# Moving GpSimd's row transfers behind the context of the next batch, in a gated cross-attention and linear kernel on one core

## Chip, cores and metric

One core of one Trainium2 chip runs the whole kernel. The metric is the device time of an execution in microseconds. TensorE is PE in the profile, VectorE is DVE, ScalarE is ACT, GpSimd is POOL and SyncE is SP.

## What is computed

All arrays are float32 but the packed weight. x has 8 batches of 100 rows of 2048, the context 8 batches of 722 rows of 2048. The weight has 2048 rows of 1536 int32 words, three words for four 6-bit values.

```
a = einsum(layernorm(x), ctx)            # per batch: 100 x 722 scores
c = einsum(softmax(a), ctx)              # 100 x 2048
x = x + tanh(g_xattn) * c
w = (unpack6(qweight) - zero_point) * scale
y = einsum(layernorm(x), w) + bias       # 800 rows x 2048 x 2048
out = x + tanh(g_ffn) * y
```

## The kernel before

The first part runs over the 8 batches, the second over 4 column blocks of the weight with 7 row tiles each. Every engine has its instruction order written out by hand, with semaphores between them.

**The batches.** The context of a batch is six tiles of up to 128 rows in `raw[:, b % 2]`, 5.9 MB together, so the context of batch b goes where that of batch b-2 was. `scores(b)` on TensorE has 32 steps f = 0 to 31: it transposes a 128-column piece of three context tiles (fill f of kind "S"; steps 0 to 15 use tiles 0 to 2, steps 16 to 31 tiles 3 to 5), and three steps later multiplies the piece, split by ScalarE (L421) and VectorE (L666) into two parts, with the queries. `attend(i)` multiplies the probabilities with the context, tile by tile (t = 0 to 5, eight matmuls each), and counts `s_pvt` after each of the first five. SyncE waits for that count and then loads the same tile of batch i+2 (L233), the last one after `s_pv`. Between the tiles t = 4 and t = 5 of `attend(i)` stand the transposes of the queries of batch i+2 (`queries`, halves (0, 1) before t = 4 and (2, 3) before t = 5). For one i the order on TensorE is `scores(i+1)`, `probs(i)`, `attend(i)`.

**The rows of x.** One buffer `xa` holds the rows of x to be normalized as queries, one buffer `xres` the rows of x to which the attention is added, one buffer `rows` the centred and scaled result for the second part. GpSimd moves them all on its own queue (q0), 800 KB a time: `next_x(b)` fetches x[b] to `xa` once the queries of batch b-1 are transposed; `x1_out(i)` sends `xres` once `residual(i)` is done; `next_xres(i)` fetches x[i] to `xres` once `x1_out(i-1)` has landed and `ln2_center(i-1)` has read it; `rows_out(i)` sends `rows`, `rs_out(i)` a column of 100 single floats. Between them it computes the reciprocal square roots (`rstd`, six small instructions).

**VectorE** in round i: `residual(i-1)`, `context_lo(i+1)` (the splits of the scores), `row_max(i+1)`, `ln2_stats(i-1)` (waits for nothing new), `ln2_center(i-1)` (L569; it writes `rows`, and so waits until `rows_out` of all batches up to i-2 has landed: `dve.wait_ge(s_rowsout, 16 * i)` within `ln2_center(i)`), `ln1_stats(i+2)` (waits for x[i+2]), `coef`, `ln2_scale(i-1)` (L575), `ln1_norm(i+2)` (L537, waits for the reciprocal square root from GpSimd), `queries_lo(i+2)`.

**The passage to the second part.** In round 6 (LAST - 1) there is no batch i+2. In its place `attend(6)` has the transposes of row tiles 0 and 1 (`normed`, "x" fills) before t = 1 to 4 and of weight tile 0 (`weights(0)`, L836) before t = 5. They share two PSUM banks; a bank is free again when VectorE has done `rows_lo` for it (L588). `unpack(n)` (L607 to L612) turns the packed words of weight tile n, loaded by SyncE (L257), into values.

Of the kernel before, what the change touches and what calls it, by code (L numbers as in the profile page):

```python
# [19 lines left out]
def flamingo_block(nc, x, ctx_in, g_xattn, g_ffn, qweight, wscale, wzero, wbias, out):  # L20
# [8 lines left out]
    CH = D // P  # L29
# [7 lines left out]
    LAST = B - 1  # L37
# [17 lines left out]
    with ExitStack() as stack:  # L55
# [3 lines left out]
        def psum(name, shape):  # L59
            return stack.enter_context(nc.psum_tensor(name, shape, F32))  # L60

        def sem(name):
            return stack.enter_context(nc.semaphore(name))
# [49 lines left out]
        S = psum("S", [P, 2, 512])  # L113
# [24 lines left out]
        s_turned = [sem(f"s_turned{k}") for k in range(4)]  # L138
# [77 lines left out]
        def bank(kind, i, f):  # L216

            return FILL[kind, i, f]
# [102 lines left out]
        @block.gpsimd  # L321
        def _(pool):
            pool.memset(ident[:, :], 0.0).then_inc(s_id0, 1)
            pool.memset(ident16[:, :], 0.0).then_inc(s_id0, 1)
            pool.memset(half[:, :], -0.5).then_inc(s_half, 1)
            pool.wait_ge(s_id0, 2)
            for m in (ident, ident16):
                pool.affine_select(out=m[:, :], in_=m[:, :], compare_op=ALU.not_equal, fill=1.0,
                                   base=0, pattern=[[-1, P]], channel_multiplier=1).then_inc(s_id, 1)
            pool.memset(fold[:, :], 0.0).then_inc(s_fold, 1)  # L330
            for k in range(STRIPS):
                pool.wait_ge(s_fold, k + 1)
                pool.affine_select(out=fold[:, :], in_=fold[:, :], compare_op=ALU.not_equal, fill=1.0,
                                   base=-32 * k, pattern=[[-1, 32]], channel_multiplier=1).then_inc(s_fold, 1)
            pool.wait_ge(s_half, 1)
            done = [0]

            def rstd(k, b):

                q = done[0]  # L340
                done[0] += 1
                vt, y0, a, c = (ln[0:R, k, i:i + 1] for i in range(4))
                to = X_SCALE if k else 1.0
                pool.wait_ge(s_aggr[k], b + 1)
                pool.tensor_scalar(vt, mr[0:R, k, 1:2], EPS, None, ALU.add).then_inc(s_var, 1)
                pool.wait_ge(s_var, q + 1)
                pool.tensor_tensor(y0, vt, half[0:R, :], ALU.pow).then_inc(s_pow, 1)
                pool.wait_ge(s_pow, q + 1)
                pool.tensor_tensor(a, y0, y0, ALU.mult).then_inc(s_nt, 1)
                pool.wait_ge(s_nt, q * 3 + 1)  # L350
                pool.tensor_tensor(a, a, vt, ALU.mult).then_inc(s_nt, 1)
                pool.wait_ge(s_nt, q * 3 + 2)
                pool.tensor_scalar(c, a, -0.5 * to, 1.5 * to, ALU.mult, ALU.add).then_inc(s_nt, 1)
                pool.wait_ge(s_nt, q * 3 + 3)
                pool.tensor_tensor(mr[0:R, k, 1:2], y0, c, ALU.mult).then_inc(s_rstd[k], 1)

            def next_x(b):
                f = bank("q", b - 1, 3)
                pool.wait_ge(s_turned[f[0]], f[1] + 1)
                pool.dma_start(xa[0:R, :], x[b]).then_inc(s_xa, 16)  # L360

            def x1_out(i):
                pool.wait_ge(s_x1, i * NCH + NCH)
                pool.dma_start(x1_dram[i], xres[0:R, :]).then_inc(s_x1out, 16)

            def rs_out(i):
                pool.wait_ge(s_rs, i + 1)
                if i == LAST:
                    pool.wait_ge(s_rsout, 16 * LAST)
                pool.dma_start(rs_dram[i * R:(i + 1) * R, :], rsum[0:R, i % 2:i % 2 + 1]).then_inc(s_rsout, 16)  # L370

            def rows_out(i):
                pool.wait_ge(s_rows, i + 1)
                pool.dma_start(rows_dram[i * R:(i + 1) * R, :], rows[0:R, :]).then_inc(s_rowsout, 16)

            def next_xres(i):
                pool.wait_ge(s_x1out, 16 * i)
                pool.wait_ge(s_mid, i)
                pool.dma_start(xres[0:R, :], x[i]).then_inc(s_xres, 16)

            rstd(0, 0)
            pool.dma_start(xres[0:R, :], x[0]).then_inc(s_xres, 16)
            next_x(1)
            rstd(0, 1)
            for i in range(B):
                if i + 2 < B:
                    next_x(i + 2)
                if i >= 1:
                    x1_out(i - 1)
                    rstd(1, i - 1)  # L390
                if i + 2 < B:
                    rstd(0, i + 2)
                if i >= 1:
                    next_xres(i)
                    rows_out(i - 1)
                    rs_out(i - 1)
            x1_out(LAST)
            rstd(1, LAST)
            rows_out(LAST)
            rs_out(LAST)  # L400
# [120 lines left out]
        def _(dve):  # L521
# [18 lines left out]
            def row_max(b):  # L540
                dve.wait_ge(s_scores, b + 1)
                dve.tensor_reduce(soft[0:R, b % 2, 0:1], S[0:R, :, 0:GW], AX.XY, ALU.max, negate=True).then_inc(s_nmax, 1)
# [9 lines left out]
            def residual(i):  # L552
                dve.wait_ge(s_xres, 16 * i + 16)
                dve.wait_ge(s_coef, i + 1)
                for n in range(NCH):
                    dve.wait_ge(s_pv, i * NCH + n + 1)
                    piece = xres[0:R, n * 512:(n + 1) * 512]
                    dve.scalar_tensor_tensor(out=piece, in0=pv[n][0:R, :], scalar=soft[0:R, i % 2, 3:4], in1=piece,
                                             op0=ALU.mult, op1=ALU.add).then_inc(s_x1, 1)
# [21 lines left out]
            def rows_lo(m, half):  # L581

                r = MROWS[m]
                for f in (2 * half, 2 * half + 1):
                    k, u = bank("x", m, f)
                    dve.wait_ge(s_hi, 4 * m + f + 1)
                    hi, lo = (xT[m][:, h, 4 * f:4 * f + 4, :] for h in range(2))
                    dve.tensor_tensor(lo, T[k][:, :].rearrange("p (c r) -> p c r", r=r), hi, ALU.subtract).then_inc(s_free[k], 1)  # L588
# [7 lines left out]
            def unpack(n):  # L596

                dve.wait_ge(s_w[n % 2], 16 * (n // 2) + 16)
                if n == 0:
                    dve.wait_ge(s_pvt, (LAST - 1) * (NT - 1) + 3)  # L600
                if 2 <= n < 2 * RT + 2:
                    k, u = bank("W", n - 2, 1)
                    dve.wait_ge(s_turned[k], u + 1)
                elif n >= 2 * RT + 2:
                    dve.wait_ge(s_wn, n - 2 - 2 * RT + 1)
                p = wraw[n % 2].bitcast(U16).rearrange("p (g w h) -> p g w h", w=3, h=2)
                dve.tensor_scalar(unp[n % 2][:, 1, :], p[:, :, 0, 0], 6, 63, ALU.logical_shift_right,  # L607
                                  ALU.bitwise_and).then_inc(s_u1, 1)
                for j, w in ((0, 0), (2, 1), (3, 2)):
                    dve.tensor_scalar(unp[n % 2][:, j, :], p[:, :, w, 0], 63, 0x6400, ALU.bitwise_and, ALU.bitwise_or)  # L610
                dve.wait_ge(s_u1, n + 1)
                dve.tensor_scalar(unp[n % 2][:, 1, :], unp[n % 2][:, 1, :], 0x6400, None, ALU.bitwise_or).then_inc(s_u, 1)  # L612
# [67 lines left out]
            for i in range(B):  # L680
                if i >= 1:
                    residual(i - 1)
                if i < LAST:
                    context_lo(i + 1, {})
                    row_max(i + 1)
                if i >= 1:
                    ln2_stats(i - 1)
                    ln2_center(i - 1)
                if i + 2 < B:
                    ln1_stats(i + 2)  # L690
                if i < LAST:
                    coef(i + 1)
                    if i >= 1:
                        ln2_scale(i - 1)
                if i + 2 < B:
                    ln1_norm(i + 2)
                    queries_lo(i + 2)
                elif i < LAST:
                    rows_lo(0, 0)
                    rows_lo(0, 1)  # L700
                    scale_and_bias()
                    unpack(0)
                    rows_lo(1, 0)
                    unpack(1)
                    rows_lo(1, 1)
            unpack(2)
            rows_lo(2, 0)
            ln2_scale(LAST - 1)
# [232 lines left out]
```

## Time and profile before

| what | value |
|---|---|
| time before, median of 3 runs | 670.11 us (667.25 to 682.67) |
| the profiled execution's own time | 668.26 us |
| its span | 666.5 us |
| PE busy | 607.7 us, 91% of the span |
| DVE, ACT, POOL busy | 392.8, 195.7, 58.2 us |
| granted TensorE clock, mean | 0.972 |
| DMA | 113.64 MB, mean 171 GB/s |

The span begins with the first instruction of the program and ends with the last, so 1.8 us of the profiled execution lie outside of it. Busy time of an engine is what its instructions took; PEld is TensorE's weight load, which overlaps its matmuls. The granted clock is the share of TensorE's full 2.4 GHz that it was given.

### The profile page before, as it was taken

The numbers are of one execution on the slowest core, as the hardware profiler recorded it, in microseconds if no ns is written. First come the engines' busy times: TensorE is split into PE (matmuls) and PEld (weight loads), VectorE is DVE, ScalarE is ACT, GpSimd is POOL, SyncE is SP. The second block draws the span as 40 slices with busy tenths as digits, with TensorE's granted clock in tenths as the row PEclk, the third lists the DMA queues.
The fourth block names the chain that finished last, engine by engine and source line by source line (L and its number), as shares of the span: only waits on it lengthen the run. The fifth ranks groups of instructions, "written<-read, shape, count | busy, mean of one in ns | idle before, by whom it ended". The sixth has DMA issues, their size and how long they took to land.

```text
span 666.5 us, 8134 instructions
## 1 busy us (share of the span) xinstructions
PE 607.7 (91%) x3240; PEld 392.1 (59%) x3240; DVE 392.8 (59%) x687; ACT 195.7 (29%) x391; POOL 58.2 (9%) x149
## 2 busy tenths in 40 slices
PE   0978999999699699969959998989999999999997
PEld 0877947947665694756559478445466444444443
DVE  2575636666375456728536675957676776563543
ACT  1544514514332350422235044223232131121000
POOL 3000000030013003001200300201200000000000
PEclk9997999999799899979989999989999999999999
DMA  8993058059829607912950692676843499394220
GB/s 250 273 285 101 1 162 282 12 180 255 308 68 305 181 0 217 266 71 87 302 165 1 226 299 106 210 220 185 285 157 83 143 252 253 90 247 106 83 68 35
DMA packets 39618, 113.64 MB, mean 171 GB/s; under 512 B 20974, under 2 KB 20974, under 8 KB 29422
## 3 DMA queue, kind: packets, MB, share of 16 engines
q1 hardware_dynamic: 18718, 83.54, 40.6%
q0 software_dynamic: 4224, 25.40, 12.7%
q10 hardware_dynamic: 16640, 4.20, 3.8%
q8 instruction: 25, 0.41, 0.3%
q14 instruction: 11, 0.09, 0.0%
HBM read 89.26 MB, written 19.66 MB: 163 GB/s over the span
## 4 chain that ended last, share of the span: by engine, by line
PE 77%; DMA 19%; DVE 2%; ACT 1%; SPq 1%; issue 1%; DVEq 0%
PE pv L812 24%; DMA raw<-in_ctx 17%; PE pv L863 17%; PE S L793 9%; PE S L863 8%; PE T L754 8%; PE S L795 5%; PE pv L754 4%; DMA raw<-in_L_ffn_qweight 2%; PE T L836 1%; PE S L876 1%; PE pv L876 1%; SPq L233 0%; ACT pT L435 0%; DVE stats L524 0%
## 5 line engine op out<-in xcount | busy, mean ns | idle before, releaser
L812 PE MATMUL pv<-raw,pT 128*100 128x512 f32 (+1 forms) x384 | 171.6, 597 | 2.5 <-ACT pT L436 2.5
L793 PE MATMUL S<-khi,qT 128*100 128x362 f32 x512 | 146.3, 368 | 0.0
L812 PEld LDWEIGHTS pv<-raw,pT 128*100 128x100 f32 (+1 forms) x384 | 62.3, 168 | 89.6 <-issue 85.8
L666 DVE TENSOR_TENSOR klo<-T,khi 128x361 fp32r<-128x361 f32 x128 | 67.7, 533 | 68.5 <-ACT khi L421 67.9
L754 PE MATMUL T<-ident,raw 128*128 128x128 f32 (+1 forms) x384 | 64.6, 284 | 31.7 <-DMA raw<-in_ctx 30.6
L421 ACT ACTIVATE khi<-T 128x361 fp32r<-128x361 f32 x128 | 60.0, 473 | 98.0 <-PE T L754 97.8
L795 PE MATMUL S<-klo,qT 128*100 128x362 f32 x256 | 87.3, 341 | 0.6 <-DVE klo L666 0.6
L666 DVE TENSOR_TENSOR klo<-pv,khi 128x361 fp32r<-128x361 f32 x128 | 67.6, 533 | 33.6 <-ACT khi L421 33.4
L754 PEld LDWEIGHTS T<-ident,raw 128*128 128x128 f32 (+1 forms) x384 | 52.3, 150 | 40.9 <-issue 37.3
L421 ACT ACTIVATE khi<-pv 128x361 fp32r<-128x361 f32 x128 | 60.0, 475 | 41.8 <-PE pv L754 41.3
L793 PEld LDWEIGHTS S<-khi,qT 128*100 128x100 f32 x512 | 71.6, 175 | 0.1
L863 PE MATMUL pv<-raw 128*128 128x512 f16 x288 | 64.0, 379 | 0.0
L754 PE MATMUL pv<-ident,raw 128*128 128x128 f32 (+1 forms) x384 | 61.7, 274 | 0.0
L754 PEld LDWEIGHTS pv<-ident,raw 128*128 128x128 f32 (+1 forms) x384 | 51.3, 146 | 3.4
L414 ACT ACTIVATE qT<-T 128x400 fp32r<-128x400 f32 x32 | 14.7, 501 | 114.9 <-PE T L754 114.9
L863 PEld LDWEIGHTS pv<-raw 128*128 128x128 f16 x288 | 28.1, 98 | 32.4
L795 PEld LDWEIGHTS S<-klo,qT 128*100 128x100 f32 x256 | 44.0, 172 | 2.5 <-DVE klo L666 2.1
L656 DVE TENSOR_TENSOR qT<-T,qT 128x400 fp32r<-128x400 f32 x32 | 17.2, 571 | 43.7 <-ACT qT L414 43.5
L754 PE MATMUL T<-ident,xa 100*128 100x100 f32 (+2 forms) x192 | 24.5, 274 | 17.8 <-DVE xa L537 14.8
L754 PEld LDWEIGHTS T<-ident,xa 100*128 100x128 f32 (+2 forms) x192 | 22.6, 172 | 27.7 <-issue 23.4
L863 PE MATMUL pv<-raw,extra 128*128 128x512 f16 x160 | 35.0, 379 | 0.0
L647 DVE TENSOR_TENSOR raw<-pv,extra 128x512 f32<-128x512 f32 (+1 forms) x18 | 12.4, 688 | 31.0 <-PE pv L863 31.0
(88 smaller groups left out, 539.7 us busy)
## 6 DMA issues: line engine op xcount, KB each, us to landing
raw<-in_ctx SPq DMA_DIRECT2D x32, 1024.0 KB, 13.4
raw<-in_ctx SPq DMA_DIRECT2D x16, 840.0 KB, 14.9
raw<-in_L_ffn_qweight SPq DMA_DIRECT2D x16, 768.0 KB, 6.5
xres<-in_x POOLq DMA_DIRECT2D x8, 800.0 KB, 8.8
x_scratch<-xres POOLq DMA_DIRECT2D x8, 800.0 KB, 14.8
rows_scratch<-rows POOLq DMA_DIRECT2D x8, 800.0 KB, 12.6
raw<-x_scratch SPq DMA_DIRECT2D x24, 256.0 KB, 4.1
out_y<-raw SPq DMA_DIRECT2D x24, 256.0 KB, 2.5
```

Source lines behind the costliest of these rows:

```text
L414: act.activation(qT[:, 0, 4 * f:4 * f + 4, :], T[k][:, 0:4 * R].rearrange("p (c r) -> p c r", r=R), ACT.Copy).then_inc(s_qhi, 1)
L421: act.activation(khi[:, (b * 2 * CH + f) % RING, 0:GW], T[k][:, 0:GW], ACT.Copy).then_inc(s_khi, 1)
L647: dve.tensor_tensor(o[0:r, :], ACC[j % NA][0:r, :], scB[0:r, cols], ALU.mult).then_inc(s_mul, 1)
L656: dve.tensor_tensor(qT[:, 1, 4 * f:4 * f + 4, :], T[k][:, 0:4 * R].rearrange("p (c r) -> p c r", r=R), qT[:, 0, 4 * f:4 * f + 4, :].bitcas ...
L666: dve.tensor_tensor(klo[:, slot, 0:GW], T[k][:, 0:GW], khi[:, slot, 0:GW].bitcast(F32), ALU.subtract).then_inc(s_free[k], 1)
L754: last = pe.transpose(dst(T[k]), src, ident[0:n, 0:n])
L793: pe.matmul(S[0:R, g, 0:MW], qT[:, h, c, :], khi[:, slot, :], start=(c == 0 and h == 0), stop=False)
L795: last = pe.matmul(S[0:R, g, 0:MW], qT[:, 0, c, :], klo[:, slot, :], start=False, stop=(c == CH - 1))
L812: last = pe.matmul(pv[n][0:R, :], pT[0:ROWS[t], t, :], raw[0:ROWS[t], b % 2, t, n * 512:(n + 1) * 512], start=(t == 0), stop=(t == NT - 1))
L836: last = pe.transpose(T[k][:, :].bitcast(F16)[:, (c % 8) * P:(c % 8 + 1) * P], unp[n % 2][:, q, gb * P:(gb + 1) * P].bitcast(F16), ident16 ...
L863: last = pe.matmul(ACC[j % NA][0:r, :], xT[m][:, h, c, :], WT[nb % 2][:, c, :], start=(c == 0 and h == 0), stop=(c == CH - 1 and h == 1))
L876: last = pe.matmul(ACC[j % NA][32 * k:32 * k + TAIL, :], xT[MT - 1][:, h, c + k, :], WT[nb % 2][:, c + k, :], start=(c == 0 and h == 0), s ...
```

## The change

GpSimd gets a wait, `context_there(b)`, until TensorE has made the transposes of fill 16 (CH is 16) of the context of batch b, the first that read the tiles 3 to 5. It stands at the head of every round i below 7, for batch i+1, ahead of `next_x(i + 2)`. `rows_out` moves from the end of its round to the next round, behind `x1_out`, for batches 0 to 4; those of 5, 6 and 7 stay in their rounds. `next_xres(i)` moves ahead of `rstd(0, i + 2)`. On VectorE the second half of `rows_lo` of row tile 1 moves ahead of `unpack(1)`.

```diff
+            def context_there(b):
+                k, u = bank("S", b, CH)
+                pool.wait_ge(s_turned[k], u + 1)
...
             for i in range(B):
+                if i < LAST:
+                    context_there(i + 1)
                 if i + 2 < B:
                     next_x(i + 2)
                 if i >= 1:
                     x1_out(i - 1)
+                if 2 <= i < LAST:
+                    rows_out(i - 2)
+                if i >= 1:
                     rstd(1, i - 1)
+                    next_xres(i)
                 if i + 2 < B:
                     rstd(0, i + 2)
+                if i >= LAST - 1:
+                    rows_out(i - 1)
                 if i >= 1:
-                    next_xres(i)
-                    rows_out(i - 1)
                     rs_out(i - 1)
...
                     unpack(0)
                     rows_lo(1, 0)
+                    rows_lo(1, 1)
                     unpack(1)
-                    rows_lo(1, 1)
```

## Rows read from the trace of the kernel before

**Rows 1.** The page's chain that ended last, by engine.

```profile
PE 77%; DMA 19%; DVE 2%; ACT 1%; SPq 1%; issue 1%; DVEq 0%
```

**Rows 2.** Waits of PE: engine, line, waited for, us in total, times, longest.

```profile
PE T L754 <- DMA raw<-in_ctx: 30.6, 6, 7.0
```

**Rows 3.** Windows between `attend` starts: us, busy by engine, granted clock, DMA share, GB/s.

```profile
85.61:134.69 49.08, 48.77 (x265) 34.95 (x263) 26.89 (x50) 18.32 (x43) 2.78 (x8) 1.00 0.47 155
...
306.55:364.77 58.22, 50.89 (x265) 36.62 (x263) 33.21 (x59) 18.32 (x42) 7.42 (x17) 0.94 0.52 158
364.77:416.60 51.83, 48.95 (x265) 34.86 (x263) 33.13 (x59) 18.32 (x42) 6.89 (x16) 1.00 0.63 203
sum 330.99, PE 301.37 PEld 216.22 DVE 192.66 ACT 109.94 POOL 39.34; mean PE 50.23 PEld 36.04 DVE 32.11 ACT 18.32 POOL 6.56
```

**Rows 4.** Timeline of PE in `scores`: start, us; idle before and releaser in brackets.

```profile
224.60 0.47 PE L754 MATMUL pv<-ident,raw 128*128 128x128 f32 x3
231.19 0.84 PE L754 MATMUL T<-ident,raw 128*128 128x128 f32 x3 [5.62 <-DMA raw<-in_ctx]
...
401.66 0.50 PE L754 MATMUL T<-ident,raw 128*128 128x128 f32 x3 [2.57 <-DMA raw<-in_ctx]
```

**Rows 5.** DMA issues by windows (56, 108, 204 and 213.5 us): KB, us to landing.

```profile
xa<-in_x POOLq DMA_DIRECT2D x1, 800.0 KB, 5.2
...
raw<-in_ctx SPq DMA_DIRECT2D x1, 840.0 KB, 8.3
...
rows_scratch<-rows POOLq DMA_DIRECT2D x1, 800.0 KB, 15.3
rs_scratch<-rsum POOLq DMA_DIRECT2D x1, 0.4 KB, 16.5
...
raw<-in_ctx SPq DMA_DIRECT2D x1, 840.0 KB, 16.9
```

**Rows 6.** Windows chosen for the DMA rate, columns as in rows 3.

```profile
111.00:114.00 3.00, 3.00 (x25) 2.92 (x24) 2.18 (x5) 1.67 (x5) 0.00 (x0) 1.00 0.93 257
210.00:215.00 5.00, 5.00 (x28) 2.87 (x25) 3.85 (x7) 1.58 (x4) 0.54 (x1) 1.00 0.99 401
215.50:222.50 7.00, 7.00 (x54) 6.77 (x54) 5.07 (x11) 4.17 (x10) 0.26 (x1) 1.00 0.91 151
229.20:236.00 6.80, 4.81 (x20) 4.51 (x21) 1.49 (x3) 1.42 (x3) 0.00 (x0) 0.50 0.03 10
...
424.50:431.00 6.50, 6.50 (x28) 3.79 (x27) 5.40 (x9) 1.99 (x4) 0.79 (x2) 1.00 0.92 289
432.50:439.00 6.50, 5.86 (x20) 2.65 (x18) 1.66 (x5) 1.08 (x2) 0.00 (x0) 1.00 1.09 150
```

**Rows 7.** Timeline of one round (i = 2), PE, DVE and POOL.

```profile
188.45 0.47 PE L754 MATMUL pv<-ident,raw 128*128 128x128 f32 x3
...
194.64 2.35 DVE L569 TENSOR_SCALAR_CACHE_REDUCE rows<-xres,mr 100x2048 f32<-100x2048 f32 x1
...
199.42 0.26 DVE L526 BATCH_NORM_AGGREGATE mr<-stats 100x2 f32<-100x24 f32 x1
...
204.71 0.54 POOL L370 DMA_DIRECT2D rs_scratch<-rsum  x1
...
210.82 0.54 POOL L360 DMA_DIRECT2D xa<-in_x  x1 [5.58 <-PE T L754]
...
215.22 0.54 POOL L364 DMA_DIRECT2D x_scratch<-xres  x1 [3.86 <-DVE xres L558]
```

**Rows 8.** Timeline of round 6, around the first weight tile.

```profile
434.76 3.60 PE L812 MATMUL pv<-raw,pT 128*100 128x512 f32 x8
437.96 0.50 DVE L607 TENSOR_SCALAR raw<-raw 128x512 uint16<-128x512 uint16 x1 [4.84 <-DMA raw<-in_L_ffn_qweight]
...
440.63 1.69 PE L836 MATMUL T<-ident,raw 128*128 128x128 f16 x16 [2.27 <-DVE extra L588]
...
442.11 4.70 PE L812 MATMUL pv<-raw,pT 105*100 105x512 f32 x8
```

## The prediction, made before the changed kernel was run

> **What bounds the kernel now.** I read the chain of waits first: TensorE holds 77% of it and DMA 19%, nobody else more than 2% [rows 1]. The list of PE's waits then names the DMA: 30.6 us in six waits for the context, the longest 7.0 us [rows 2]. To see where they lie I cut the batch part into windows from the start of one `attend` to the start of the next [rows 3]. The reader is to compare them: every window has the same 265 matmuls, the first takes 49.08 us, the fifth 58.22, the sixth 51.83. The timeline shows what the long ones hold [rows 4]: TensorE does 16 steps of `scores`, finds tiles 3 to 5 not there at step 16, and stands still for 5.62 us (7.0 in the worst window, 2.57 in the sixth). After the longer stops the granted clock is 0.50 for 6.8 us, 1.2 GHz instead of 2.4 [rows 6]; after the 2.57 us stop it stays 1.00 through its window [rows 3, 4].
>
> What an undisturbed round costs follows from the sixth window: 51.83 - 2.57 = 49.26 us, with the row work of VectorE in it. The sum of all six is 330.99 [rows 3]; less the first (49.08) this is 281.91, and five undisturbed rounds are 246.3. So **35.6 us** hang on late tiles, clock included: for the fifth, 58.22 - 49.26 = 9.0, of which 7.0 standing and 2.0 slow clock.
>
> Why are the tiles late? The last tile of the context comes 16.9 us after its issue in a late round and 8.3 us in the round with no wait, and 5.2 is what 800 KB need alone [rows 5]. TensorE reaches step 16 some 12.2 us after the start of `scores` (213.4 to 225.6, [rows 4]). Two things lie in the way. GpSimd's queue has xres, rows, xa and x_scratch in flight exactly then (issued up to 215.2, the last two at 210.8 and 215.2, [rows 7]), 3.3 MB beside the context's 5.9 MB. And for 7 us the DMA engines are as busy as before (0.91) but move 151 GB/s instead of 401 [rows 6]. That stretch comes when the 100 single floats of `rs_out` are under way, issued at 204.71 and landed 16.5 us later [rows 5, 7]. I put it on them and not on the `scores` phase, since it comes again at 432.5 to 439 within an `attend` (150 GB/s), and is missing in the `scores` of the first round, which has no `rs_out` (257 GB/s) [rows 6].
>
> **The change part by part.** The new wait ends at step 16 of `scores(i+1)`, by when all six tiles have landed. I count from there. Fifteen more steps of 0.81 us end at 12.2; `ln2_center`, the first to need anything, starts 194.64 - 188.92 = 5.7 us after the last transposes [rows 7], at 17.9.
>
> *The wait and what is queued behind it.* Behind it on GpSimd stand `next_x`, `x1_out`, `rows_out` and then the square roots, which need VectorE's statistics from after `scores` anyway. The three issues take 0.54 us each [rows 7], from 0.3 to 1.9. Lower bound for the third landing: 5.2 us for the first, and two more at 289 GB/s, the rate of two queued transfers [rows 5, 6], 2 x 2.8: 11.1. Upper bound: issued at 1.4 and as slow as the slowest shown, 15.3 [rows 5]: 16.7. I take 12, near the low end, since the context is all in and the queue is alone. Both ends are ahead of 17.9, so the new dependence of `ln2_center(i-1)` on `rows_out(i-2)` costs nothing; its cover is 1.2 to 6.8 us. If it were gone, each us would shift the query transposes, with little slack of their own. x[i+2] lands first and is needed later still. In round 0 x[2] is fetched later than before too, and needed as late as in the others. In round 2 the three broadcast loads of 1 MB go out behind context 3 on SyncE's queue; they are through within some 8 us (3.1 MB at 401 GB/s), about when the three transfers start.
>
> *What leaves the context's way.* x, x1 and rows, 2.5 of the 3.3 MB, go into a stretch of idle DMA. What remains is `next_xres(i)`. It now goes right after `ln2_center` has read xres (194.64 + 2.35 = 197.0 in the round of rows 7; before, some 1.7 us ahead of the issue at 204.71), and `rs_out` right behind the square root of x[i+2], at some 203.0. The single floats then follow 0.8 MB instead of 1.6 MB and no x1 or x. So the slow stretch moves from 215.5 to 222.5 to about 205 to 212, into `attend`. Tiles 0 to 2 (3.0 MB) must land by 213.4, the end of `attend`. By 205 the context has 1.8 to 2.4 MB in (8 us at 289 to 401 GB/s, less 0.8 for xres), in the slow stretch 1.06 MB more (7 us at 151): 2.9 to 3.4. So tile 2 lands between in time and, if it needs what follows the stretch, 1 us late. I take 0.5 us in five rounds: **+2.5** (0 to 5). Tiles 3 to 5: at 212 at most 3.1 MB are missing, 7.7 us at 401; with the usual 1 us for landing, 221, against a need at 225.6. So no wait at step 16, and no fall of the clock. The whole **35.6 us** go.
>
> The Trainium skill (DMA: Bandwidth & Descriptors, Specifications) says that transfers under 512 bytes are read-modify-write; it does not say that they slow others. If the slow stretch were not theirs but that of `scores`, it would stay at 215.5, with 1.3 MB left then: 8 us at 151 GB/s, in time too; the sum would lose its +2.5.
>
> *`next_xres` ahead of `rstd(0)`.* Its issue takes up to 1.2 us, and ends before VectorE has the statistics of x[i+2], 199.42 against 197.0 + 1.2 [rows 7]. Nothing on the path; xres lands long before `residual`.
>
> *Rounds 6 and 7.* The sends of round 5 keep their place, and `rows_out(4)` lands before `ln2_center(5)` as above. Nothing.
>
> *VectorE's exchange.* Before, TensorE ended tile t = 4 at 438.36 and stood 2.27 us until `rows_lo(1, 1)`, which stood behind `unpack(1)`, which waited 4.84 us for the weight [rows 8]. Now `rows_lo` goes 4 us earlier, and `unpack(1)` waits as before, 0.65 us later if at all, with weight tile 1 needed only in the next `attend`. After its stop TensorE had the half clock: 4.70 us instead of 3.60 for eight matmuls and some 0.6 more on the transposes [rows 8]. Together **3.9 us** (2.3 to 3.9, if the clock falls anyway).
>
> **Sum.** 668.26 - 35.6 - 3.9 + 2.5 = 631.3 us against the profiled execution; its own 668.26 is 1.9 below the median of the three runs, so I say **632 us**, 5.7% faster.
>
> **The rivals.**
> (1) *The wait moves to the start of `scores`.* The single floats now slow the first tiles. If xres and the floats take all of the DMA from 198 to 212, tile 2 comes 3 us late in five rounds, and the clock falls in each (2 us): 631.3 - 2.5 + 25 = 654. For it: 1.8 MB at the low end is only just enough. Against: 300 GB/s and more in `attend` otherwise.
> (2) *The x traffic was not the cause.* The sixth window has no fetch of x and no late rows, and still waits 2.57 us. If as much stays in five rounds: 644. Against: there the slow stretch still lay on tiles 3 to 5, and now moves away.
> (3) *Slower: GpSimd's burst ends after `ln2_center` wants it.* VectorE then holds back x[i+2] and the queries, and TensorE stands in `attend` with a fallen clock. It decides from a third landing at 17.9 plus 1.5 us of slack. To cost more than the 39.5 us gained, five rounds would have to lose 8 us each (6 standing and 2 clock), a third landing at 25: three transfers at about 105 GB/s. Only if the burst itself brings on the slow rate: some 680 us at 27. Against: 289 GB/s for two such transfers in a row.
> (4) *The change doesn't do what it says*, because the wait ends early: it can't, since step 16 reads the tiles that it stands for. Part of (2).
>
> **Chances.** Forecast (624 to 641) 0.72, (2) 0.10, (1) 0.14, (3) 0.02, and something better, a round below 49.26 us, 0.02. The range from 624 to 648 takes in the forecast's unknowns (+2.5 at 0 to 5, the exchange's 1.6, some 3 us from execution to execution) and (2); it leaves out (1) and (3). About 2% is what a measurement tells from no change, 13 us here, which all but (3) exceed: faster 0.95, same 0.03, slower 0.02.
>
> **What would show it.** The list of waits should have only the first load of PE's waits for the context; windows from `attend` to `attend` of 49 to 50 us with the clock at 1.00; issues of xa, x_scratch and rows_scratch one behind the other in the middle of `scores`; landing of the context's last tile 6 to 9 us after issue; the low-rate stretch in the middle of `attend`; no wait of L836 for L588. It would be wrong if a wait stands before the first transposes of `scores` (1), at step 16 (2), or before the query transposes (3).

## The result, and the profile after

The changed kernel took 636.8 us (median of 4, 631.6 to 648.2) against 669.7 us before: a ratio of 0.950, 95% interval 0.937 to 0.962. Run twice more on other occasions it gave 0.946 (0.941 to 0.951) and 0.944 (0.938 to 0.951), with medians of 638.7 and 639.7 us where the kernel before took 676.6 and 677.2 us. Medians are of all executions of a kernel, ratios leave out those that are over 1.5% above the fastest of it. The forecast was 632 us, range 624 to 648, a ratio of 0.943.

The execution that was profiled first (648.2 us) has two waits of 5.3 and 7.6 us in the second part for weight tiles transposed by DMA, which the two later profiles of the same kernel don't have; what lengthened them isn't shown. So I read the later one of 637.4 us span, and call it the second profile.

The page's chain that ended last, of the second profile:

```profile
PE 83%; DMA 13%; DVE 1%; ACT 1%; SPq 1%; issue 1%; DVEq 0%
```

The waits of PE, in the same profile (us in total, times, longest):

```profile
PE T L765 <- DVE xa L548: 15.6, 1, 15.6
PE T L765 <- DMA raw<-in_ctx: 10.8, 6, 5.8
```

30.6 us of waiting for context have become 10.8 [rows 2]. Of these, 2.8 before and 6.7 now are the first load, ahead of any round (the 5.8 is part of it): in the rounds 27.8 us have become 4.1. DMA's share of the chain goes from 19% to 13% [rows 1]. The wait of L836 for L588 is gone. Windows from the start of one `attend` to the next, as in rows 3, with the granted clock and the DMA rate last:

```profile
92.42:141.51 49.09, 48.78 (x263) 34.97 (x263) 26.88 (x50) 18.30 (x43) 2.77 (x8) 1.00 0.48 155
141.51:191.75 50.24, 48.96 (x262) 34.84 (x262) 33.18 (x59) 18.29 (x43) 7.77 (x17) 1.00 0.80 247
191.75:242.47 50.72, 48.97 (x263) 34.87 (x263) 33.19 (x59) 18.30 (x43) 7.77 (x17) 1.00 0.61 182
242.47:291.93 49.46, 48.98 (x263) 34.86 (x263) 33.18 (x59) 18.29 (x43) 7.79 (x17) 1.00 0.63 187
291.93:342.10 50.17, 48.96 (x262) 34.85 (x262) 33.19 (x59) 18.30 (x43) 7.79 (x17) 1.00 0.64 184
342.10:392.13 50.03, 48.96 (x262) 34.88 (x262) 33.18 (x59) 18.30 (x43) 7.25 (x16) 1.00 0.71 210
392.13:418.55 26.42, 26.11 (x102) 13.37 (x103) 20.95 (x37) 7.98 (x17) 3.70 (x9) 1.00 0.78 215
```

The first window is as before; the next five were 56.5, 57.2, 58.2, 58.2 and 51.8 us and are now 49.5 to 50.7, with the clock at 1.00 throughout. Their sum is 250.6 instead of 281.9. The last line is round 6 with the first weight tile: 26.42 us, where the kernel before has this, from its own `attend(6)` to its `attend(7)`:

```profile
417.13:447.65 30.52, 27.94 (x103) 14.30 (x103) 20.83 (x37) 7.98 (x17) 3.72 (x9) 0.94 0.77 226
```

So 31.3 + 4.1 us are gained, the second part takes the same 218.8 us in both, and 6.3 us are lost in the first 92 us (the first `attend` starts at 92.4 instead of 86.1), where both kernels do the same: TensorE waits 3.9 us longer for the first load, and the granted clock of the stretch is 0.93 instead of 0.96. In the third profile it starts at 85.8, so this changes from execution to execution.

**The three transfers.** The timeline of POOL from `attend(2)` into the next `scores` (start us, us), and under it the landings of the DMAs issued between 227.5 and 229 us (KB, us to landing):

```profile
202.71 1.47 POOL L375 DMA_DIRECT2D rs_scratch<-rsum  x1
227.81 0.55 POOL L365 DMA_DIRECT2D xa<-in_x  x1 [23.63 <-PE T L765]
228.35 0.53 POOL L369 DMA_DIRECT2D x_scratch<-xres  x1
228.87 0.53 POOL L379 DMA_DIRECT2D rows_scratch<-rows  x1
```

```profile
xa<-in_x POOLq DMA_DIRECT2D x1, 800.0 KB, 6.3
x_scratch<-xres POOLq DMA_DIRECT2D x1, 800.0 KB, 8.0
rows_scratch<-rows POOLq DMA_DIRECT2D x1, 800.0 KB, 9.6
```

They go out one behind the other in the middle of `scores`; the third lands at 228.87 + 9.6 = 238.5, 10.6 us after the first issue. The reader sees where it is needed in VectorE's timeline, which starts L580 (`ln2_center`, L569 before) 6.9 us later, with no wait in front:

```profile
244.99 0.27 DVE L537 BATCH_NORM_AGGREGATE mr<-stats 100x2 f32<-100x24 f32 x1
245.38 2.35 DVE L580 TENSOR_SCALAR_CACHE_REDUCE rows<-xres,mr 100x2048 f32<-100x2048 f32 x1
```

**What is left.** TensorE still waits, not at step 16 of `scores` but at its first transposes:

```profile
164.72 0.50 PE L765 MATMUL T<-ident,raw 128*128 128x128 f32 x3 [0.98 <-DMA raw<-in_ctx]
215.42 0.82 PE L765 MATMUL T<-ident,raw 128*128 128x128 f32 x6 [1.44 <-DMA raw<-in_ctx]
```

The low-rate stretch has moved with the single floats, as the windows of DMA rate show (GB/s last):

```profile
203.00:209.00 6.00, 6.00 (x22) 2.82 (x21) 2.13 (x3) 0.90 (x2) 1.19 (x1) 1.00 1.00 354
210.00:216.00 6.00, 4.56 (x21) 2.16 (x20) 3.87 (x6) 0.94 (x3) 0.00 (x0) 1.00 0.62 91
```

So 354 GB/s until 209, then 91 until 216. The floats were issued at 202.7. GpSimd's queue moves 24 packets under 512 bytes between 208 and 210 and none from 210 to 217: the low rate follows on the small packets and doesn't run beside them. The third context tile (index 2) was issued just before them, and these are its landing (window 202.2 to 202.6) and theirs:

```profile
raw<-in_ctx SPq DMA_DIRECT2D x1, 840.0 KB, 12.8
```

```profile
rs_scratch<-rsum POOLq DMA_DIRECT2D x1, 0.4 KB, 12.6
```

202.33 + 12.85 (the tile's time in the chain) = 215.2 and 202.71 + 12.6 = 215.3: tile and floats land together, and TensorE, ready for the tile, stood for 1.4 us. By 209 the context queue had moved some 3.3 MB, more than the 3.0 MB of tiles 0 to 2. So a count of bytes doesn't explain the late tile. Whether its last packets or only the word of their arrival came late isn't shown.

### The profile page after: what moved, and what is told of

It reads as the page before. It is cut to its first block, busy times and chain, and to the rows that moved or that the text cites. A ratio compares the mean times of both kernels' runs of the same rounds, so it can differ in the third digit from the quotient of the medians.

```text
span 646.4 us, 8141 instructions
## 1 busy us (share of the span) xinstructions
PE 601.2 (93%) x3240; PEld 385.5 (60%) x3240; DVE 392.9 (61%) x687; ACT 195.7 (30%) x391; POOL 60.1 (9%) x149
## 4 chain that ended last, share of the span: by engine, by line
PE 81%; DMA 16%; DVE 1%; ACT 1%; SPq 1%; issue 1%; DVEq 0%
PE pv L823 19%; PE pv L874 17%; PE S L804 12%; DMA raw<-in_ctx 12%; PE T L765 9%; PE S L874 8%; PE S L806 6%; PE pv L765 6%; DMA raw<-xa 3%; PE T L847 1%; PE S L887 1%; PE pv L887 1%; SPq L233 1%; ACT pT L446 0%; DVE stats L535 0%
## 5 line engine op out<-in xcount | busy, mean ns | idle before, releaser
L804 PE MATMUL S<-khi,qT 128*100 128x362 f32 x512 | 142.8, 360 | 0.0
L806 PE MATMUL S<-klo,qT 128*100 128x362 f32 x256 | 85.8, 335 | 0.6 <-DVE klo L677 0.6
L804 PEld LDWEIGHTS S<-khi,qT 128*100 128x100 f32 x512 | 69.6, 170 | 0.1
L765 PE MATMUL T<-ident,raw 128*128 128x128 f32 (+1 forms) x384 | 61.9, 275 | 7.3 <-DMA raw<-in_ctx 6.1
L765 PEld LDWEIGHTS T<-ident,raw 128*128 128x128 f32 (+1 forms) x384 | 50.6, 145 | 15.9 <-issue 12.5
L806 PEld LDWEIGHTS S<-klo,qT 128*100 128x100 f32 x256 | 42.7, 167 | 2.3 <-DVE klo L677 2.0
L874 PE MATMUL pv<-raw,extra 128*128 128x512 f16 x160 | 36.8, 392 | 7.6 <-DMA raw<-xa 7.6
L477 ACT ACTIVATE xa<-raw 128x2048 f16<-128x2048 f16 x8 | 15.3, 1910 | 63.0 <-DVE raw L623 63.0
```

The source lines that it names most:

```text
L477: act.activation(wn[n % 2], unp[n % 2].rearrange("p j g -> p (j g)").bitcast(F16), ACT.Copy, bias=-float(BIAS16)).then_inc(s_wn, 1)
L765: last = pe.transpose(dst(T[k]), src, ident[0:n, 0:n])
L804: pe.matmul(S[0:R, g, 0:MW], qT[:, h, c, :], khi[:, slot, :], start=(c == 0 and h == 0), stop=False)
L806: last = pe.matmul(S[0:R, g, 0:MW], qT[:, 0, c, :], klo[:, slot, :], start=False, stop=(c == CH - 1))
L874: last = pe.matmul(ACC[j % NA][0:r, :], xT[m][:, h, c, :], WT[nb % 2][:, c, :], start=(c == 0 and h == 0), stop=(c == CH - 1 and h == 1))
```

## The experiments

Ratios are against the kernel before, run on the same chip in the same job, with 95% intervals.

**after_again** and **after_third**: the changed kernel again.

> The changed kernel as it is, for a profile without the long transposes of the second part and for a closer ratio. My theory: 632 us, ratio 0.944 (0.935 to 0.955), windows from attend to attend of 49 to 50 us with the granted clock at 1.00; the waits at the start of the second weight block (5.3 and 7.6 us in the first profile) were an accident of that execution. Rival: these waits come with the change, because the second part now starts at another moment; then 645 us, and they stand in this profile too.

> The changed kernel again, beside the three others on this chip, for comparison: 632 us, ratio 0.944.

Measured 0.946 (0.941 to 0.951) and 0.944 (0.938 to 0.951). The waits in the second part are in neither profile. The third profile shows how much the waits at the start of `scores` vary, here in three of its rounds:

```profile
134.89:187.57 52.68, 50.41 (x262) 36.33 (x263) 33.30 (x59) 18.50 (x43) 7.77 (x17) 0.97 0.79 235
...
239.22:289.80 50.58, 48.98 (x262) 34.88 (x262) 33.20 (x59) 18.29 (x43) 7.79 (x17) 1.00 0.65 183
289.80:344.00 54.20, 50.44 (x262) 36.14 (x262) 33.21 (x59) 18.30 (x43) 7.78 (x17) 0.97 0.64 170
```

The waits in these rounds are 2.0, 1.3 and 3.5 us, and behind the first and the last the granted clock is 0.50 for three to four us. So the half clock has not gone for good with the change.

**swap_only**: VectorE's exchange alone.

```diff
                     rows_lo(1, 0)
+                    rows_lo(1, 1)
                     unpack(1)
-                    rows_lo(1, 1)
```

> The kernel before with only VectorE's exchange: rows_lo(1, 1) ahead of unpack(1). My theory: no wait of L836 for L588 in round 6, 2.3 to 3.9 us less, ratio 0.994 to 0.997. Rival: the wait moves to the next weight load and nothing is gained, ratio 1.000.

Measured 0.995 (0.991 to 0.998), 3.6 us less at 669, as expected and just clear of no change. Its round 6:

```profile
424.75:451.16 26.41, 26.11 (x102) 13.36 (x102) 20.76 (x37) 7.97 (x17) 3.71 (x9) 1.00 0.80 202
```

26.41 against 30.52: 4.1 us, with the clock at 1.00 instead of 0.94. The wait for L588 is gone and no other came. This profile also shows how much the kernel before varies: its five rounds with waits take 287.6 us together, where those of rows 3 take 281.9.

**wait_only**: the new wait alone, in the kernel before.

```diff
             for i in range(B):
+                if i < LAST:
+                    context_there(i + 1)
                 if i + 2 < B:
                     next_x(i + 2)
```

> The kernel before with only the new wait at the head of GpSimd's round: x and x1 move behind the context, rows_out, next_xres and rs_out stay where they were. My theory: 1.6 MB leave the context's way, the slow stretch of the single floats stays at the start of scores; the last tile lands 9 to 11 us after its issue, just about in time: 0 to 2 us of waiting per round, 632 + 4 to 646 us, ratio 0.950 to 0.965. Rival (the x traffic was not the cause, the single floats were): the wait at step 16 stays at some 5 us, 660 us, ratio 0.985.

Measured 0.961 (0.955 to 0.967), in my range but with less gained than its middle; the rival's 0.985 is excluded. Its waits of PE:

```profile
PE T L761 <- DMA raw<-in_ctx: 16.4, 6, 3.3
PE T L843 <- DVE extra L595: 3.3, 1, 3.3
```

Without the first load these are 13.4 us in five rounds, 2.7 each at step 16, more than the 0 to 2 expected; the second line is what the exchange takes away.

**late_wait**: the changed kernel with the wait at the last transposes of the context.

```diff
-                k, u = bank("S", b, CH)
+                k, u = bank("S", b, 2 * CH - 1)
```

> The changed kernel with the wait 15 steps later, at the last transposes of the context (fill 31 in place of 16), so that the cover of the three transfers is gone. My theory: the third transfer lands about 12 us later, 6 us after ln2_center could start; with 1.5 us of slack the query transposes come 5 us late and the clock falls (2 us) in four rounds, and 2 to 3 us in round 6: 660 us (650 to 672), all the gain but 10 us given back, ratio 0.985. Rival (the moment does not matter as long as the context is in): 632 us, ratio 0.945.

Measured 0.989 (0.983 to 0.996): most of the gain is given back. The profiled execution took 676.5 us, the three others 664.7 to 669.5. Its timelines of DVE and PE in round 3 show the mechanism; the second PE line is of round 4, the third of round 6:

```profile
262.49 2.35 DVE L580 TENSOR_SCALAR_CACHE_REDUCE rows<-xres,mr 100x2048 f32<-100x2048 f32 x1 [7.74 <-DMA rows_scratch<-rows]
```

```profile
271.96 1.26 PE L765 MATMUL T<-ident,xa 100*128 100x100 f32 x6 [6.01 <-DVE xa L548]
328.41 0.93 PE L765 MATMUL T<-ident,xa 100*128 100x100 f32 x4 [4.98 <-DVE xa L548]
...
435.19 0.98 PE L765 MATMUL T<-ident,xa 128*128 128x128 f32 x5 [2.07 <-DVE extra L599]
```

`ln2_center` waits 7.7 us for `rows_out`, and TensorE 5.3, 6.0, 5.0 and 6.5 us for the queries in the four rounds (2.1 in round 6). The four waits are 22.8 us together. So the dependence that the change creates is real, and hidden by the place of the wait.

**order_only**: the changed kernel without the new wait.

```diff
             for i in range(B):
-                if i < LAST:
-                    context_there(i + 1)
                 if i + 2 < B:
```

> The changed kernel without the new wait: rows_out a batch later, next_xres earlier, VectorE's exchange, but x and x1 fetched and sent as early as before. My theory: x, x1 and rows (2.5 MB) now all lie on tiles 4 and 5; they wait 2 to 5 us at step 16 in most rounds, with a fall of the clock: 645 to 662 us, ratio 0.965 to 0.99. Rival (the gain came from the slow stretch alone, which this kernel moves too): 632 to 636 us, ratio 0.95.

Measured 0.958 (0.949 to 0.966), a little better than expected. It waits both at the start of `scores` and at step 16, in some rounds at both:

```profile
PE T L763 <- DMA raw<-in_ctx: 16.7, 7, 3.4
```

Beside after_third (0.944, same job) the wait itself is worth 1.4%, some 9 us; the two intervals just overlap, and every execution of after_third is faster than every one of order_only, the closest by 1.3 us.

**before_singles** and **after_singles**: the kernel before, and the changed one, with the single floats of batches 0 to 6 in one transfer after batch 6.

```diff
-        rsum = sb("rsum", [P, 2])
+        rsum = sb("rsum", [P, B])
...
-                pool.dma_start(rs_dram[i * R:(i + 1) * R, :], rsum[0:R, i % 2:i % 2 + 1])
+                if i == LAST - 1:
+                    pool.dma_start(rs_dram[0:LAST * R, :].rearrange("(b r) o -> r (b o)", r=R), rsum[0:R, 0:LAST], ...)
```

> The kernel before, with the single floats of batches 0 to 6 sent in one transfer after batch 6 and no longer in each round (the sums are kept in eight columns; all is still computed). My theory: the stretch of 150 GB/s at the start of scores is gone, the last context tile lands 10 to 12 us after its issue, in time or nearly: 633 to 645 us, ratio 0.95 to 0.965. Rival (the slow stretch belongs to scores or to the x traffic, not to the single floats): it stays, 668 us, ratio 1.00.

> The changed kernel with the single floats of batches 0 to 6 in one transfer after batch 6. My theory: the low rate in the middle of attend goes, tile 2 is in time, the two waits of 0.7 and 1.0 us at the start of scores go: 630 us, ratio 0.942, within 2 us of the changed kernel. Rival (the single floats do nothing): the low-rate stretch stays and the time is the same as that of the changed kernel.

Measured 0.952 (0.945 to 0.960), as expected, and 0.924 (0.915 to 0.933), better than the 0.942 that I expected: I took the floats' cost in the changed kernel from the two short waits of the first profile. The 0.924 rests on two executions, 625.2 and 626.1 us; the two others took 640.5 and 644.4, for a reason that no profile shows. In before_singles `attend(2)` starts 4.3 us earlier than in the kernel before, so the stretch that had 151 GB/s [rows 6] corresponds to this one, with 256:

```profile
211.20:218.20 7.00, 7.00 (x54) 6.77 (x54) 5.07 (x11) 4.19 (x10) 0.26 (x1) 1.00 0.93 256
```

The waits for context are halved, from 30.6 to 14.3 us. In after_singles no round waits any more; all five are 49.05 to 49.09 us, and only the first load is left in the list:

```profile
230.97:280.06 49.09, 48.79 (x262) 34.94 (x262) 33.20 (x59) 18.29 (x43) 6.43 (x16) 1.00 0.57 188
280.06:329.14 49.08, 48.77 (x262) 34.93 (x262) 33.20 (x59) 18.30 (x43) 6.43 (x16) 1.00 0.57 188
...
PE T L766 <- DMA raw<-in_ctx: 1.7, 1, 1.7
```

The 700 floats, once sent together in the last round, make a low-rate stretch there, 46 GB/s for 7 us (8 in all by windows of 1 us, and 9 in before_singles) and 411 after it, under work that does not wait:

```profile
422.00:429.00 7.00, 7.00 (x36) 3.40 (x34) 4.68 (x8) 3.80 (x4) 0.00 (x0) 1.00 0.92 46
430.00:434.00 4.00, 4.00 (x27) 2.11 (x26) 3.70 (x8) 0.00 (x0) 0.71 (x2) 1.00 0.99 411
```

**after_double**: the floats sent twice.

```diff
                 pool.dma_start(rs_dram[i * R:(i + 1) * R, :], ...).then_inc(s_rsout, 16)
+                if i < LAST:
+                    pool.dma_start(rs_copy[i * R:(i + 1) * R, :], ...).then_inc(s_rscopy, 16)
```

> The changed kernel, with the single floats of batches 0 to 6 sent twice, the second time to an array that nobody reads. My theory (the writes of 100 single floats hold up all DMA engines for some 7 us): the low-rate stretch becomes about twice as long, tile 2 lands 5 to 7 us later, and TensorE waits that much longer at the start of scores in five rounds, with a fall of the clock: 30 to 45 us more than the changed kernel, 670 to 685 us, ratio 0.99 to 1.01. Rival (the stretch has a fixed length, whatever is sent): the same as the changed kernel, 0.945.

Measured 0.948 (0.941 to 0.954): my expectation fell, the rival's stands. The tile and both transfers land together again, 12.1, 11.9 and 10.6 us after issues at 201.3, 201.7 and 203.2:

```profile
raw<-in_ctx SPq DMA_DIRECT2D x1, 840.0 KB, 12.1
```

```profile
rs_scratch<-rsum POOLq DMA_DIRECT2D x1, 0.4 KB, 11.9
rs_copy<-rsum POOLq DMA_DIRECT2D x1, 0.4 KB, 10.6
```

```profile
210.00:216.00 6.00, 5.33 (x27) 3.04 (x25) 4.95 (x9) 1.69 (x5) 0.00 (x0) 1.00 0.59 108
```

100 and 200 floats make one stretch of some 7 us, 700 floats one of 8 to 9. The cost hangs on there being such a transfer, and little on how many floats it has.

**after_wide**: each float as the first of a row of 512 bytes.

```diff
-        rs_dram = nc.dram_tensor("rs_scratch", (B * R, 1), F32, kind="Internal").ap()
+        rs_dram = nc.dram_tensor("rs_scratch", (B * R, P), F32, kind="Internal").ap()
...
-        rsum = sb("rsum", [P, 2])
+        rsum = sb("rsum", [P, 2, P])
```

> The changed kernel, with each of the 100 single floats sent as a row of 512 bytes (127 zeros beside it): the same number of pieces on the same queue at the same moment, each 128 times as large. My theory (it is the size of the piece): no low-rate stretch, no waits at the start of scores, as with the floats deferred: ratio 0.925. Rival (it is the write to DRAM of 100 scattered pieces, whatever their size): the waits stay, ratio 0.945.

Measured 0.937 (0.927 to 0.947), less than the 0.925 that I expected; the rival's 0.945 lies within the interval, so the time alone doesn't decide. The profile does. PE's list holds the first load alone (2.3 us), all rounds are 49.04 to 49.09 us, and tile and floats land 7.0 and 6.8 us after issue instead of 12.8 and 12.6. `attend(2)` starts 8.0 us earlier than in the second profile, so this window corresponds to 211 to 217 there:

```profile
203.00:209.00 6.00, 6.00 (x33) 3.98 (x32) 5.81 (x11) 2.18 (x7) 0.00 (x0) 1.00 0.84 292
```

The same 100 pieces at the same place in the queue no longer make the stretch. Two things have changed with them: each piece is 128 times as large, and they go to places 512 bytes apart in DRAM where the floats lay 4 bytes apart, within 400 bytes. Which of the two does it isn't shown; single floats sent 512 bytes apart would tell.

**order_singles** and **wait_singles**: with the floats deferred, the changed kernel without the wait, and the kernel before with the wait and the exchange.

> The changed kernel without the new wait and with the single floats deferred. Without the low-rate stretch the x traffic beside the context may be harmless. My theory: 2.5 MB still lie on tiles 4 and 5, which land 9 to 12 us after their issue; 0 to 1 us of waiting per round: 626 to 634 us, ratio 0.925 to 0.937. Rival (the wait is needed whatever the floats do): 2 to 3 us per round, ratio 0.95, as the kernel before with the floats deferred.

> The kernel before with the new wait, VectorE's exchange and the floats deferred, but rows_out and next_xres where they were. My theory: xres and rows (1.6 MB) beside the context fit in; no wait at step 16, the same as the changed kernel with the floats deferred: ratio 0.924 to 0.93, so that the later rows_out is worth nothing once the floats are gone. Rival: 1.6 MB beside the context still cost 1 to 2 us per round, ratio 0.935 to 0.94.

Measured 0.936 (0.928 to 0.943) and 0.936 (0.930 to 0.942). The first is in my range; the second has the ratio of its rival, but not the rival's waits of 1 to 2 us per round. Order_singles has no wait in any round, and wait_singles none for context (two of its rounds take 50.0 and 49.3 us). With the floats out of the way either part of the change does, and the intervals of the four kernels without context waits overlap or touch; what remains between them is mostly the start, 83.8 us to the first `attend` in after_singles and 85.6 to 87.4 in the others.

## Why the prediction was right

*What bounded the kernel.* Right, and shown from both sides: with all context waits gone a round takes 49.07 us, 0.2 less than the 49.26 that I took as undisturbed. The half clock went with the stops in the rounds of the first two profiles; in the third it came back in two rounds, once behind a wait of only 2.0 us, which I had not allowed for. The 6.8 us at 0.50 in my reading begin 2.0 us before the stop ends (229.2 against 231.2), so some 4.8 us of work ran at that clock.

*Two causes of the late tiles.* Right. Taking away the x traffic alone (wait_only) gives 0.961, the floats alone (before_singles) 0.952, both 0.924 to 0.937 (with the exchange, which is 0.995 alone). Rival (2) falls with wait_only. That the slow stretch belongs to the floats, which I inferred from two windows, is shown by before_singles, after_singles and after_wide.

*The cover of the new dependence.* Right in mechanism. The third transfer landed 10.6 us after the first issue, 10.9 after the wait's end, just under my lower bound of 11.1. That it came so close is luck in part: the first transfer took 6.3 us and not 5.2, and the next two followed by 2.2 us each and not 2.8 (my 289 GB/s was of a window that held traffic of another queue too). The three broadcast loads, which I had through in some 8 us, landed 12 to 18 us after their issue and lay beside the three transfers of their round, whose third landed at 189.4, still 5.3 us ahead of `ln2_center`. late_wait shows the price without the cover, 5.0 to 6.5 us per round. Rival (3) would have needed far slower transfers.

*`rs_out` moved into `attend`: the term that was mis-sized.* I had +2.5 us (0 to 5), from a slow stretch at 205 to 212, over before tile 2 is needed at 213.4. In the second profile it lies from 210 to 217, seven us after the issue instead of two, and tile 2 lands within it although the queue had moved more than its bytes before. My step from bytes moved to the landing failed there. It also had a slip: 8 us at 289 GB/s less 0.8 MB are 1.5 MB and not 1.8. The context had 2.0 MB in at 205, within either range, so it is the place of the stretch that was wrong. Against 49.07 us per round the five rounds lost 3.2, 5.3 and 13.7 us in the three profiles. This is rival (1), at less than its price of 25 us. The Trainium skill (DMA: Bandwidth & Descriptors, Queues, rings and completion order) says that a completion is written only after every earlier write of that DMA engine, across its queues. Here tile and floats landed within 0.2 us of each other in all 13 rounds with such a wait in the three profiles, now one ahead and now the other, which agrees with it; that it is this and not the low rate that delays tile 2 was argued, not shown.

*The exchange.* 4.1 us in the round, 3.6 us in the time, against 3.9.

*The sum.* 31.3 + 4.1 = 35.4 us gained in the batch part of the second profile, against 35.6 + 3.9 - 2.5 = 37.0. The 5 us between 632 and the first median are the larger term of tile 2 (in the third profile 11 us more than I took) and the first load, which moved the first `attend` between 84 and 92 us and is in no step of mine. That the ratios of the later jobs, 0.946 and 0.944, meet the 0.943 of the forecast so closely is luck in part. I took what the rounds lose before from one execution of 668 us: 36.6 us against rounds of 49.07; in the profile of swap_only (672 us), which is the kernel before up to round 6, they lose 42.2. So I sized the saving too small by several us, and the term of tile 2 as well.

## What to carry to other kernels

When two streams share the DMA engines, cut the profile into equal rounds and compare the landing time of the same tile in the slow and the undisturbed one; then ask of each transfer beside it when its result is needed, and send it in the stretch where the engines are idle, with the cover counted in us before its first reader. A transfer of single floats can cost more than one of 800 KB: look for windows with busy DMA engines and a low rate, and send such data wide, late or together. In this kernel that was worth about 5% by itself, as much as reordering the large transfers.

## What was not expected of the hardware

- A store of 100 single floats to DRAM is followed by some 7 us in which both queues together move 91 to 151 GB/s, where they reach 400. 200 floats make it no longer (108 GB/s), 700 floats make 8 to 9 us (46 GB/s), and 100 pieces of 512 bytes make none (292 GB/s).
- The stretch begins late and not always at once: 7 to 9 us after the issue in the changed kernel, 11 us in the kernel before, where more is queued.
- The tile issued just before the floats on another queue lands with them, within 0.2 us.
- Why the length hardly depends on the number, and whether the size of the pieces or their distance in DRAM matters, stays open.
